# Splitting the experts' weights in 57 of the 64 steps of the attention loop

## The reference, cut to what matters

```python
x = x + xattn(layernorm(x), ctx, ...)      # 16 heads, latent projections, rope, window of 8 keys
x = x + moe(layernorm(x), gate_w, w_gate, w_up, w_down)
x = x + memory_attention(layernorm(x), ctx, mask)
x = x + ffn(layernorm(x), ...)             # dense MLP and a product-key memory

def moe(h, ...):
    scores = softmax(h @ gate_w.T); topk_w, topk_idx = top_k(scores, 6)     # 16 experts
    for e in range(16):
        y = y + cw[:, e:e+1] * ((silu(h @ w_gate[e].T) * (h @ w_up[e].T)) @ w_down[e].T)
```

## Time and profile before

| | us |
|---|---|
| three runs | 1923.48, 1925.89, 1927.55 |
| median | 1925.89 |
| the profiled execution | 1932.41 |
| its span, first to last instruction | 1930.6 |
| TensorE busy in the span | 1815.8 (94%) |
| VectorE, ScalarE, GpSimd busy | 1092.1, 879.5, 818.2 |

### The profile page before, as it was taken

The page is one execution under the profiler, slowest core; times in us unless marked ns, Lnnn a source line. Parts: engine busy times, 40 slices in busy tenths (PEclk is TensorE's granted clock), DMA queues, the critical chain, the costliest instruction groups (busy, mean ns, idle before and its releaser), DMA issues.

```text
span 1930.6 us, 39335 instructions
## 1 busy us (share of the span) xinstructions
PE 1815.8 (94%) x12853; PEld 1083.2 (56%) x12853; DVE 1092.1 (57%) x2536; ACT 879.5 (46%) x1833; POOL 818.2 (42%) x731
## 2 busy tenths in 40 slices
PE   7989999999962999999999999995899999999998
PEld 4566666666631666666666666663654444444444
DVE  5577888888862323322223232233657777777776
ACT  5478878888841443434344344342742221122211
POOL 5134456666663334443443434432112444544442
PEclk9999999999985999999999999997999999999999
DMA  8255588888896666666666665555002355555553
GB/s 319 77 161 170 181 151 181 186 175 169 185 167 163 154 147 141 154 166 145 145 147 150 153 152 101 95 90 129 33 34 59 130 189 197 206 175 205 206 176 144
DMA packets 156351, 294.80 MB, mean 153 GB/s; under 512 B 41248, under 2 KB 91040, under 8 KB 152032
## 3 DMA queue, kind: packets, MB, share of 16 engines
q1 hardware_dynamic: 105184, 157.48, 31.0%
q0 software_dynamic: 46368, 126.29, 26.4%
q10 hardware_dynamic: 4608, 8.52, 1.6%
HBM read 426.00 MB, written 78.33 MB: 261 GB/s over the span
## 4 chain that ended last, share of the span: by engine, by line
PE 69%; DMA 11%; DVE 10%; ACT 4%; issue 4%; POOL 1%; SPq 1%; POOLq 0%; another core or an unknown queue 0%; ACTq 0%; DVEq 0%
PE bank L235 18%; PE bank L237 18%; PE bank L236 18%; DMA x_sum<-x,work_arena 7%; DVE work_arena L1575 2%; PE bank L1060 2%; PE bank L850 1%; PE bank L1087 1%; DMA x<-token_rows,work_arena 1%; DVE xt_arena L1575 1%; ACT xt_arena L1313 1%; PE bank L928 1%; PE bank L1171 1%; DMA work_arena<-in_moe_w 1%; DMA expert_tokens<-work_arena 1%
## 5 line engine op out<-in xcount | busy, mean ns | idle before, releaser
L235 PE MATMUL bank<-work_arena,xt_arena 128*128 x1221 | 404.8, 332 | 2.8 <-DVE xt_arena L2063 1.9
L237 PE MATMUL bank<-work_arena,xt_arena 128*128 x1221 | 404.7, 331 | 0.0
L236 PE MATMUL bank<-work_arena,xt_arena 128*128 x1221 | 404.7, 331 | 0.0
L2302 POOL DMA_INDIRECT x_sum<-x,work_arena x111 | 177.1, 1595 | 397.9 <-DMA x_sum<-x,work_arena 192.9
L2051 DVE TENSOR_TENSOR xt_arena<-xt_arena,bank 128x352 f32<-128x352 f32 x111 | 57.9, 521 | 407.1 <-PE bank L237 407.1
L235 PE MATMUL bank<-work_arena 128*128 128x512 f16 (+1 forms) x600 | 226.0, 378 | 12.8 <-DVE x L1874 6.8
L236 PE MATMUL bank<-work_arena 128*128 128x512 f16 (+1 forms) x600 | 225.9, 378 | 0.0
L237 PE MATMUL bank<-work_arena 128*128 128x512 f16 (+1 forms) x600 | 225.7, 378 | 0.0
L1465 ACT ACTIVATE xt_arena<-bank 128x1024 f16<-128x1024 f16 x111 | 113.7, 1024 | 230.0 <-PE bank L1060 230.0
L235 PE MATMUL bank<-xt_arena,work_arena 128*128 128x512 f16 x528 | 200.1, 379 | 1.8 <-DVE xt_arena L195 1.8
L236 PE MATMUL bank<-xt_arena,work_arena 128*128 128x512 f16 x528 | 200.1, 379 | 0.0
(11 more groups left out here) (278 smaller groups left out, 3872.6 us busy)
## 6 DMA issues: line engine op xcount, KB each, us to landing
work_arena<-expert_w SPq DMA_DIRECT2D x111, 1408.0 KB
work_arena<-expert_w SPq DMA_DIRECT2D x111, 768.0 KB
work_arena<-in_moe_w SPq DMA_DIRECT2D x64, 352.0 KB
expert_w<-work_arena SPq DMA_DIRECT2D x128, 176.0 KB
work_arena<-in_moe_w SPq DMA_DIRECT2D x64, 192.0 KB
expert_w<-xt_arena SPq DMA_DIRECT2D x128, 96.0 KB
work_arena<-in_mlp_w SPq DMA_DIRECT2D x8, 1536.0 KB, 9.0
work_arena<-in_head_w SPq DMA_DIRECT2D x16, 512.0 KB, 6.4
```

Of the source, the lines that this page charges most:

```text
L235: pe.matmul(o, a_hi, b_hi, start=start, stop=False)
L236: pe.matmul(o, a_hi, b_lo, start=False, stop=False)
L237: return pe.matmul(o, a_lo, b_hi, start=False, stop=stop)
L2302: pool.indirect_dma_start(out=xacc[:, :], out_offset=bass.IndirectOffsetOnAxis(ap=rid[:, i:i + 1], axis=0), in_=ysb[:, b % YB, :], in_offs ...
```

## The change

`pieces_of` spreads the 128 pieces evenly over 57 steps instead of giving two to each of the 64: piece i belongs to step i * 57 // 128. A step then has two or three pieces, and steps 57 to 63 have none. VectorE takes all but the first piece of a step early in the next one, and the call behind the loop is gone.

```diff
+SPLIT_STEPS = 57
...
         def pieces_of(m):
-            return [(i, i % NPC) for i in (2 * m, 2 * m + 1) if 0 <= i < E * NPC]
+            return [(i, i % NPC) for i in range(E * NPC) if i * SPLIT_STEPS // (E * NPC) == m]
...
-            def split_dve(m, which):
-                for i, q in pieces_of(m)[which:which + 1]:
+            def split_dve(m, late):
+                for i, q in pieces_of(m)[1:] if late else pieces_of(m)[:1]:
                     n, s = PIECES[q][1], i % STAGES
                     dve.wait_ge(split_hi, i + 1)
                     lo_of(sp_lo[s][:, 0:n], sp32[s][:, 0:n], WS, sp_hi[s][:, 0:n]).then_inc(split_lo, 1)
...
-            split_dve(STEPS - 1, 1)
             add_outputs(14)
```

## The result

Twelve runs of each kernel, taken in turn on one chip, gave 1931.69 us for the changed kernel (1925.81 to 1940.38) and 1926.2 us for the one before (1920.23 to 1929.88). The ratio is 1.003, with an interval of 1.0017 to 1.0043: 5.5 us slower, where 10.7 us faster was forecast. The profiled execution of the changed kernel took 1930.08 us, that of the kernel before 1932.41 us. The two profiled executions thus don't show the difference as a whole. The kernel before was caught in an execution above all of its twelve timed runs, and one of its rows, as we shall see, was unusually long.

What follows compares the result with a forecast made beforehand. TensorE was taken to bound the attention loop, tied with VectorE in rank steps, with late pieces and loads bounding its end. Loss 6.8 against gain 17.5, net 10.7 us, from the 1925.9 us median: 1915 us, range 1906 to 1927.

Steps and rivals of the forecast that it cites:

- step 3: In the loop, some loads go only one step ahead; ScalarE's waits cost 1 us in all, ends 0 and 25.
- step 5: Behind the loop, first expert loads go over 30 us earlier, shortening the link after the last placement: 8.5 us gain.
- step 4: At the loop's end, steps 57 to 63 lose 14 pieces and GpSimd is late next: 9.0 us gain.
- Step 1: Pieces fall into steps 0 to 56: 14 steps of three (0, 4, ..., 52), 43 of two; per piece nothing changes.
- Step 2: Third pieces on VectorE cost 4.5 us ahead of `rope_dve` in five rank steps, 1.3 us in steps 0 and 4.
- the choice of 0.89 over 1.62 us: Each rank step's third piece on VectorE takes 0.89 us, since GpSimd's pair of instructions is over by then.
- The rival that named this mechanism: Pieces starve the loop: late loads in nine patterns, steps 20 to 53, cost 25 us, giving 1939 us; chance 0.11.
- the early loads only change places: Behind the loop, early expert loads slow the placements too, so step 5 gains nothing: 1923.7 or 1926.2 us; chance 0.14.

Runs made afterwards that it cites:

- dup: Kernel before, with VectorE computing one large low part twice ahead of the rope product in five rank steps; ratio 1.0031.
- thin57: Changed kernel, with the third piece's low part in five rank steps made for one column instead of 704; ratio 1.0012.
- second pair: Repeat profiles of the kernel before and the changed kernel, both unaltered, from two chips and sets; loops 437.5 and 449.8 us, changed kernel's ratio 1.0018.
- before_again: Kernel before, run and profiled once more unchanged, in a later set; its loop up to step 60 took 437.5 us.
- held57: Changed kernel, with SP issuing the expert loads only after TensorE has done 61 steps, as late as in the kernel before; ratio 1.0019.
- cut14: Kernel before with only 114 pieces made, the last 14 filled by early copies inside DRAM; ratio 0.9942, 11.3 us faster.
- cut14_held: cut14 with SP issuing the expert loads only after TensorE has done 61 steps; ratio 0.9977.
- first60: Changed kernel with eight steps of three pieces, steps 4 to 11, two in every other step up to 59; ratio 0.9961 against the kernel before.
- first60b: Repetition of first60; ratio 0.9982 (0.9958 to 1.0006) against the kernel before.
- noload64: Kernel before, with the loads of pieces from the fifth on, and ScalarE's waits for them, left out; ratio 0.9951.
- noload57: Changed kernel, with the loads of pieces from the fifth on, and ScalarE's waits for them, left out; ratio 0.9981 against the kernel before.

## Why the prediction was wrong, step by step

Two steps failed above all: step 3, which let 1 us of ScalarE's waits through to the loop, and step 5, which counted 8.5 us for a link that the early loads hardly shorten. The sum of the terms as measured (below), with nothing for step 5, is 15.6 us worse than forecast. Step 5 has 8.5 us of this, the loop's steps 2 and 3 have 4.7 (11.5 us lost for 6.8), and step 4 has 2.4 (6.6 us gained for 9.0).

**Step 1** held: L1361 doesn't occur behind step 56, and the steps of three were 0, 4, ..., 52.

**Step 2** forecast 4.5 us for five third pieces on VectorE and 1.3 us in steps 0 and 4. Alone five more pieces cost 6.0 us by the ratio and 3.2 by the medians (dup), so the size fits, within the interval. In the changed kernel they showed less. TensorE's waits at L898 rose from 1.4 to 3.3 us, none of them above 0.75 us, and taken out the five third pieces gave 1 us (thin57). Steps 0 to 7 lost 0.6 us instead of 1.3, though the third pieces of steps 0 and 4 took 1.94 and 1.62 us, not 0.89 and 0.56. From step 8 on they took 0.88 us (large) and 0.55 us (small), so there the choice of 0.89 over 1.62 us held. What I hadn't seen is the piece ahead of them, the second of a step. In the kernel before it is always a small one; now it is a large one half of the time. The groups by shape, columns as line, engine, tiles, count, busy us, mean ns, idle time before:

```profile
L1576 DVE SCALAR_TENSOR_TENSOR work_arena<-work_arena 128x704 f16<-128x704 f32 x64 | 70.0, 1093 | 36.1 <-ACT work_arena L1361 34.6 <-issue 1.4
...
L1576 DVE SCALAR_TENSOR_TENSOR xt_arena<-work_arena,xt_arena 128x384 f16<-128x384 f32 x64 | 51.2, 801 | 29.1 <-ACT xt_arena L1361 28.8
```

Before, the large ones took 891 ns and the small ones 1005 ns on average. The sum is the same (121.2 and 121.3 us), but a large second piece takes 1.37 us in most steps where a small one took 1.04, and 1.95 us in steps 13, 21, 37 and 53 where a small one took 1.62. In the rank steps the second piece is small as before. The Trainium skill (SBUF — State Buffer, section Who interferes with whom) would lay such a long instruction to GpSimd's instruction beside it. The trace agrees: the 1.95 us in step 21 began at 249.84 us, beside a GpSimd instruction of 1.44 us from 249.60 us on, and the third piece behind it took 0.55 us. So it is the second piece that pays.

**Step 3 failed.** Its first half was near. From a landing of 7.1 us it put 1.1 and 1.7 us of ScalarE's waits on each pattern, 25 us in the nine patterns from step 20 on, and ScalarE waited 29.4 us. What failed is that I let 1 us of this through to the loop, since ScalarE has 1.26 us of idle time and TensorE leads for the next 30 us. Waits of 3 to 5 us came in one piece, after transfers of 8 to 13 us, and such a one passes through all that stands behind it. Of the 7.7 us that TensorE idles more between 237 and 531 us (9.9 - 2.2), its rows give 4.7 to ScalarE (5.2, before 0.5) and 2.8 to VectorE (3.3 + 1.2 at L898 and L972, before 1.4 + 0.3). The 1.2 us at L972 come in step 49, 2.5 us after ScalarE's longest wait for a load (4.7 us), and may be the load's too. So in the first pair the larger part is step 3's and the smaller step 2's. In the second pair TensorE's waits for ScalarE are 7.3 us more, those for VectorE 2.0 us fewer (0.7 and 2.7), and its gaps without a cause 2.9 us more. Up to step 20 the loop had lost 0.7 us, from there to step 60 10.7, of which 4.4 in steps 20 to 23. What its idle time doesn't explain of these is the granted clock, 0.99 instead of 1.00 over 294 us, up to 3 us. The 2.3 us behind the wait of 3.93 us are the most of it.

TensorE's missing idle time in the old order was taken for slack. It showed that nobody was late, not that lateness would be absorbed. The rival that named this mechanism had a chance of 0.11. Its price was 2.8 us per pattern and its point of decision 1.3. The 10.7 us in nine patterns are 1.2 us each, and 0.9 without the 2.8 us put down to VectorE. The rival was right in place and mechanism and not in size. This loss alone would have left the kernel 6 us faster (17.5 - 11.5). It took the smaller gain behind the loop as well to make it slower.

**Step 4** (9.0 us forecast, 6.5 to 10.9) came out at 6.6 us in the first pair (67.3 to 60.7) and at 6.1 us in the second (70.6 to 64.5). GpSimd is late next, as said: its timeline shows waits of 2.61 us at 549.31 us and 1.32 us at 570.49 us ahead of L2213. The 6.5 us that I called sure were all there was.

**Step 5 failed too, and by more** (8.5 us forecast). The loads go 31 us earlier as forecast, and the last token rows' store does land sooner by it. From its issue to the end of SP's wait for it took 11.8 to 20.8 us in the six profiles with late loads (20.8 in the first one, 13.6 in before_again), and 6.5 to 9.4 us in the fourteen with early ones. But SP waits for the placements too. In the changed kernel:

```profile
SPq L763 <- DMA token_rows<-xt_arena: 18.8, 1, 18.8
SPq L764 <- DMA expert_tokens<-work_arena: 6.9, 1, 6.9
```

The store's wait ended at 600.8 us instead of 607.3, and then SP waited 6.9 us for the last placement, which is issued 8.2 us behind the store and took 7.7 us itself. In the kernel before this second wait was 0.4 us. I had put 4 us for the link, from the 3.9 us of the earlier trace rows, but that is the landing of a store. No profile shows a placement's below 7.5 us, so in no run here could early loads bring the link below that. And it was 13.0 us only in the profiled execution: 8.2 us in before_again, 7.5 us in held57 with its late loads. The 4.8 us between 13.0 and 8.2 would be most of the 6.5 us by which that execution stood above the median. I had set its sum against the median but took this term from it uncorrected. The rival *the early loads only change places* is right that the link gains next to nothing, but not for its reason, since the store does land sooner. Whether the early loads help elsewhere is open: cut14 to cut14_held says 6.8 us (3.7 by the medians), the changed kernel and held57 say nothing.

**The sum** of what was measured: 11.5 us of loss in the loop (6.8 forecast) against 6.6 us of gain behind it (17.5 forecast) is 4.9 us slower; the runs say 5.5. The terms come from single profiles, so the closeness is in part luck: in the second pair the same sum is 12.3 - 6.1 = 6.2 us, and the ratio there says 3.5 us.

## What to carry to other kernels

Work that is moved out of a stretch where it is late is only free elsewhere if its buffers turn over there. Count the steps between a buffer's release and its next use, before and after. Beside the median landing, ask what a single one as late as the longest of that stretch would hold up. When two waits end together, ask how long the second takes by itself before you price the first. Move such work to where the DMA queues have room (here ahead of the first placements) and no more of it than the stalled stretch holds: eight steps of three early gained, 14 spread evenly lost. Before a single link of one execution goes into a sum, look for it in a second profile, above all where that execution is slower than the timed runs.

## What the runs showed of the hardware that was not expected

The medians of the kernel before differ between sets, from 1926 us in two of them to 1937 to 1942 us in the others, 11 to 16 us more, and by one profile of each most of it is inside the loop: 437.5 us up to step 60 in before_again instead of 421.6. The profiles of the slower sets have gaps in TensorE's head products, up to 2.6 us each, in which it waits for nothing that the profile shows. The rows of before_again, 237 to 531 us:

```profile
PE bank L898 <- issue: 3.2, 3, 1.5
PE bank L897 <- issue: 2.7, 4, 1.9
PE bank L899 <- issue: 2.4, 2, 1.9
```

The first profiles of both kernels and first60 have none of these among TensorE's products; first60b has 7.5 us. They stand in the densest runs of small products, 0.06 us each. In noload64, where the share of busy DMA falls from 0.80 to 0.38 in the stretch, they are 2.0 us instead of 9.1, but in noload57, with a share of 0.36, they are 6.8 us. So loaded queues alone don't explain them, and their cause stays open. After the longest of them the clock fell. In noload57, the table of stretches around its gap of 2.59 us:

```profile
478.00:490.00 12.00, 8.28 (x76) 5.31 (x73) 6.44 (x14) 6.31 (x17) 7.53 (x7) 1.00 0.28 55
490.00:494.00 4.00, 4.00 (x15) 2.02 (x14) 3.30 (x6) 1.35 (x3) 0.00 (x0) 0.57 0.35 114
494.00:513.00 19.00, 19.00 (x210) 13.62 (x209) 12.61 (x24) 16.53 (x46) 10.86 (x10) 1.00 0.26 89
```

TensorE was busy for 8.3 of 12 us, and then worked for 4 us at a granted clock of 0.57, near the lower of its two levels (1.2 GHz), before it was back at full. Steps 52 and 53 were 5.5 us longer than in noload64: 3.7 us of gaps, and 1.7 us for 4 us at that clock.

A store's landing depends on what goes beside it. The 264 KB of token rows took 3.9 us before the placements begin and 7.1 us (median) with them, and behind the loop 6.5 to 9.4 us with the expert loads gone early, 11.8 to 20.8 us with them beside it.

What wasn't tried: a fifth buffer, and making the last pieces behind the loop, beside the first experts, where VectorE is busy for 30% of the time (620 to 1000 us).
